# Transposes of the attention probabilities one pair at a time between the fill's matmuls, in two of a pair's four steps

## The chip, the core and the metric

The kernel runs on one core of a Trainium2 chip. The metric is the device time of one execution in microseconds (us). Before the change it is 3376.25 us, the median of 3 runs (3374.19 to 3376.97).

## What is computed

Two graph layers over x of 32 batches, each 512 rows by 512 features, all in fp32:

```python
# layer 0
y = einsum('nm,bmd->bnd', adj, x);  out = y @ weight + bias
x = layernorm(x + out)
# layer 1: masked attention with 8 heads of 64, mask = (adj == 0)
qkv  = x @ w_qkv
attn = softmax(where(mask, -inf, q @ k.T * 64**-0.5))
o    = (attn @ v) @ w_proj + b_proj
x    = layernorm(x + o + layernorm(o) * gamma + beta)
```

## The kernel before

**Number format.** Every product of two fp32 operands is done as three matmuls on parts: hi (the value rounded to fp32r) and lo (what is left), as hi·hi + hi·lo + lo·hi. ACT makes the hi parts (a copy with rounding), DVE the lo parts (a subtraction).

**Stages.** Layer 0 comes first; the first turn of layer 1 starts at 803.9 us. Layer 1 runs over 32 batches, some 79 us each. The change lies in it.

**A batch of layer 1** is four pairs of heads ("groups", 0 to 3), and each pair is four steps of 128 query rows, so a batch has 16 steps k = 0 to 15. What a step passes through, in order:

- PE `scores` (L778): q·k of both heads into `s_bank`, 6 matmuls. It stands three steps ahead: step k issues `scores(k + 3)`, which waits for `max_found` of step k + 2 (L772), since it overwrites the banks that DVE reads there.
- DVE `masked_max` (L1122): adds the mask, writes `probs` and its row maximum (`bias_row`). For step k + 2 it is issued in DVE's step k, behind `inverse(k + 1)` (L1131), which waits for `probs_turned` of step k (L1130): `probs` has two buffers, and the transposes of step k read the one that step k + 2 writes.
- ACT `exponent` (L1020), then DVE `inverse` (L1131), then POOL `normalise` (L693, L696), which counts `probs_made`.
- PE `turn` (L790 to L797): 16 transposes, in 8 pairs; the two of a pair take the upper and the lower 64 rows of the array, and write the two `t_bank`s. The last two count `probs_turned`.
- ACT `pt_hi` (L1027) and DVE `pt_lo` (L1142), two instructions each, read `t_bank`; `pt_lo` counts `ptlo_made`.
- PE `attend_v` (L813), once for the four steps of a pair: in the last step of the pair with `pt_hi`, in the first step of the next pair with `pt_lo`.

`ready_to_turn` (L783) is PE's wait before a turn: for `probs_made` of this step and `ptlo_made` of the step before. In the third and last step it stands inside `scores`, ahead of its last pair of matmuls (L775); in the first and second it stands ahead of the last matmul pair of the fill (L923).

**The fill** is work of other products that needs nothing from the current step: `v_matmuls` in group 0, `project` of the batch before in group 1, `qk_matmuls` of the next batch in groups 2 and 3. All three issue through `half_pair` (L820): one unit g is two matmuls, one in the upper and one in the lower rows of the array, lines L822 and L824. 48 units belong to a group. At g = 12 and 36 the halves of the array swap banks, so the first unit there waits until unit g - 1 is complete (L851, L872, L892). Batch 0 has no fill in group 1, the last batch none in groups 2 and 3.

PE's order is written out by hand in `batch`: the first step issues turn, matmuls with `pt_lo` and units 8 to 15, the second turn, units 16 to 25, scores, units 26 to 35, the third turn, units 36 to 47, scores, the last turn, 8 units of the next group around `pt_hi`'s matmuls, scores.

Of the kernel before, what the change touches and what calls it, by code (L numbers as in the profile page):

```python
# [18 lines left out]
def graph_layers(nc, x, adj, w0, b0, wqkv, wproj, bproj, gamma, beta, out):  # L19
    B, N, D = x.shape  # L20
    T = N // P
# [17 lines left out]
    with ExitStack() as whole:  # L39
# [474 lines left out]
        with ExitStack() as second:  # L514
# [123 lines left out]
            def pair_before(b, group):  # L638

                return (b, group - 1) if group > 0 else (b - 1, PAIRS - 1)  # L640
# [122 lines left out]
            def _(pe):  # L763
# [21 lines left out]
                    if not (isinstance(b, int) and b * STEPS + k == 0):  # L785
                        pe.wait_ge(ptlo_made, b * 32 + 2 * k)

                def turn(k):

                    for a in range(2):  # L790
                        for m in range(T):
                            for i, h in enumerate((TOP, BOTTOM)):
                                cols = slice((a * T + m) * HEAD, (a * T + m + 1) * HEAD)
                                last = pe.transpose(t_bank[i][:, cols], probs[h, k % 2, a, m * P:(m + 1) * P],  # L794
                                                    ident[h, h])
                                if a == 1 and m == T - 1:
                                    last.then_inc(probs_turned, 1)  # L797

                def attend_v(b, p, part, run):

                    first, end = part is pt_hi and run == 0, part is pt_lo and run == 0
                    if part is pt_hi and run == 0:
                        pe.wait_ge(pthi_made, b * 32 + (8 * p + 8))
                    elif part is pt_hi:
                        pe.wait_ge(pv_half, b * 16 + (4 * p + 2))
                    elif run == 1:
                        pe.wait_ge(ptlo_made, b * 32 + (8 * p + 8))
                    else:
                        pe.wait_ge(pv_half, b * 16 + (4 * p + 4))
                    for m in range(T):  # L810
                        for a, h in ((run, TOP), (1 - run, BOTTOM)):
                            w = v[h, m, 2 * p + a, :, :].rearrange("p s d -> p (s d)")
                            last = pe.matmul(o_bank[a][:], w, part[h, a, m, :], start=first and m == 0,  # L813
                                             stop=end and m == T - 1)
                            if m == T - 1 and end:
                                last.then_inc(pv_done, 1)
                            elif m == T - 1 and part is (pt_hi, pt_lo)[run]:
                                last.then_inc(pv_half, 1)
# [42 lines left out]
                def v_matmuls(b, first, count):  # L861
                    for g in range(first, first + count):
                        n, run, (m, s) = g // 24 * 2, g // 12 % 2, divmod(g % 12, 3)
                        if g % 24 == 0:
                            if isinstance(b, int) and b == 0:
                                pe.wait_ge(qklo_made, 6 + n)
                            elif n == 0:
                                pe.wait_ge(qklo_made, b * 8 + 6)
                            else:
                                pe.wait_ge(ot_summed, b * 8)  # L870
                        elif g % 12 == 0:
                            pe.wait_ge(v_half, b * 4 + (n + 2))  # L872
                        a, c = ((xt_hi, w_hi), (xt_hi, w_lo), (xt_lo, w_hi))[s]
                        pieces = half_pair([g_bank[n], g_bank[n + 1]],
                                           [a[:, m, (n + w) * P:(n + w + 1) * P] for w in range(2)],
                                           [c[:, 2, m, :]] * 2, run, g % 12 == 0, g % 12 == 11)
                        if g % 12 == 11:
                            for piece in pieces:
                                piece.then_inc(v_done if run else v_half, 1)
# [24 lines left out]
                def batch(b, last_part=True, more=True):  # L904
                    def fill(group, first, count):
                        if group == 0:
                            v_matmuls(b, first, count)
                        elif group == 1 and last_part:
                            project(b, first, count)
                        elif 2 <= group < PAIRS and more:  # L910
                            qk_matmuls(b + 1, 48 * (group - 2) + first, count)
                        elif group == PAIRS and more:
                            v_matmuls(b + 1, first, count)

                    def filled(group):
                        return group == 0 or (last_part if group == 1 else more)

                    def fill_and_wait(group, first, count, k):

                        if filled(group):  # L920
                            fill(group, first, count - 1)
                        if k < STEPS or more:
                            ready_to_turn(b + k // STEPS, k % STEPS)  # L923
                        if filled(group):
                            fill(group, first + count - 1, 1)

                    def scores_ahead(k, turn_next=False):
                        if k + 3 < STEPS or more:
                            scores(b, k + 3, (b + (k + 1) // STEPS, (k + 1) % STEPS) if turn_next else None)
                        elif turn_next and k + 1 < STEPS:  # L930
                            ready_to_turn(b, k + 1)

                    def low_outputs(b, p, between=None):
                        attend_v(b, p, pt_lo, 1)
                        if between is not None:
                            fill(*between)
                        attend_v(b, p, pt_lo, 0)

                    def first_step(k, group):
                        turn(k)  # L940
                        if group > 0 or last_part:
                            low_outputs(*pair_before(b, group), (group, 8, 2) if filled(group) else None)
                        elif filled(group):
                            fill(group, 8, 2)
                        if filled(group):
                            fill(group, 10, 2)
                        scores_ahead(k)
                        fill_and_wait(group, 12, 4, k + 1)

                    def second_step(k, group):  # L950
                        turn(k)
                        if filled(group):
                            fill(group, 16, 10)
                        scores_ahead(k)
                        fill_and_wait(group, 26, 10, k + 1)

                    def third_step(k, group):
                        turn(k)
                        if filled(group):
                            fill(group, 36, 12)  # L960
                        scores_ahead(k, turn_next=True)

                    def last_step(k, group):
                        turn(k)
                        more_fill = filled(group + 1) and (group + 1 < PAIRS or more)
                        if more_fill:
                            fill(group + 1, 0, 6)


                        if group == 0:  # L970
                            pe.wait_ge(vlo_made, b * 4 + 4)
                        elif group == 1 and last_part:
                            pe.wait_ge(o_made, b * 4)
                        elif group >= 2 and more:
                            pe.wait_ge(qklo_made, b * 8 + (4 * group + 4))
                        else:
                            pe.wait_ge(ot_summed, b * 8 + 2 * group)
                        attend_v(b, group, pt_hi, 0)
                        if more_fill:
                            fill(group + 1, 6, 2)  # L980
                        attend_v(b, group, pt_hi, 1)
                        scores_ahead(k, turn_next=True)

                    for group in range(PAIRS):
                        first_step(T * group, group)
                        second_step(T * group + 1, group)
                        third_step(T * group + 2, group)
                        last_step(T * group + 3, group)
                    if not more:
                        low_outputs(b, PAIRS - 1)  # L990
# [313 lines left out]
```

## Time and profile before

| | before |
|---|---|
| median of 3 runs | 3376.25 us |
| the profiled execution, its own time | 3375.78 us |
| its span, first to last instruction | 3374.0 us |
| PE, busy share of the span | 98% |
| DVE | 78% |
| ACT | 66% |
| POOL | 59% |
| mean granted clock of TensorE | 0.989 of 2.4 GHz |

Each row of the timeline gives a start and a duration in us from the span's start; instructions of one kind in a row are merged into one. Starts of PE's matmuls are when they are taken up, their ends are modelled: two matmuls that follow each other overlap in the rows. A step's length on PE is therefore read from the start of one turn to the start of the next.

### The profile page before, as it was taken

How to read it: one execution, taken by the hardware profiler on the slowest of the kernel's cores; microseconds unless marked ns; L12 is line 12 of the kernel's file. 1: busy time of each engine (PE TensorE's matmuls, PEld its weight loads, DVE VectorE, ACT ScalarE, POOL GpSimd, SP SyncE). 2: the span in 40 equal slices, each digit the busy share in tenths (PEclk: the TensorE clock that was granted, in tenths of full speed). 3: DMA queues.
4: the chain of work that ended last, by engine and by line, in shares of the span. 5: the costliest groups of instructions: out<-in, count | busy, mean ns of one | idle time of the engine just before them, and what ended most of it. 6: DMA issues, size and time to landing. Idle time of an engine off the chain costs nothing.

```text
span 3374.0 us, 87933 instructions
## 1 busy us (share of the span) xinstructions
PE 3308.7 (98%) x31760; PEld 2938.4 (87%) x31760; DVE 2623.3 (78%) x6430; ACT 2224.8 (66%) x4629; POOL 1991.9 (59%) x2686
## 2 busy tenths in 40 slices
PE   8999999998999999999999999999999999999995
PEld 6888888886899998999899999999999999999994
DVE  7666666664788888888888888888888888888886
ACT  4444444444677777777777777777777777777774
POOL 4555556552466666666666656666666666666665
PEclk9999999998999999999999999999999999999997
DMA  5565565553011111111122111111111111112210
GB/s 187 174 195 169 183 190 171 186 173 108 27 51 51 54 54 51 51 54 51 51 69 69 55 51 51 51 51 51 54 54 51 51 54 51 51 57 69 68 39 32
DMA packets 345168, 279.61 MB, mean 83 GB/s; under 512 B 13664, under 2 KB 275808, under 8 KB 344928
## 3 DMA queue, kind: packets, MB, share of 16 engines
q1 hardware_dynamic: 344928, 275.83, 26.8%
q8 instruction: 222, 3.64, 0.4%
q14 instruction: 18, 0.15, 0.0%
HBM read 141.56 MB, written 134.22 MB: 82 GB/s over the span
## 4 chain that ended last, share of the span: by engine, by line
PE 75%; issue 13%; POOL 9%; DVE 1%; ACT 0%; DMA 0%; SPq 0%; POOLq 0%; DVEq 0%
PE bank L822 34%; PE bank L813 15%; PE bank L778 10%; PE bank L824 9%; PE bank L794 7%; POOL xb L282 5%; POOL ub L276 4%; PE bank L319 0%; POOL rstd L287 0%; DVE probs L1122 0%; DVE o_stats L1168 0%; DVE pt_lo L1142 0%; DMA x_lo<-ut_lo 0%; ACT pt_hi L1027 0%; POOLq L279 0%
## 5 line engine op out<-in xcount | busy, mean ns | idle before, releaser
L1027 ACT ACTIVATE pt_hi<-bank 128x512 fp32r<-128x512 f32 x1024 | 556.4, 596 | 548.7 <-PE bank L794 536.0
L1020 ACT ACTIVATE probs<-probs,bias_row 128x512 f32<-128x512 f32 x1024 | 731.5, 720 | 44.8 <-DVE bias_row L1122 43.6
L1142 DVE TENSOR_TENSOR pt_lo<-bank,pt_hi 128x512 fp32r<-128x512 f32 x1024 | 657.6, 684 | 41.4 <-PE bank L813 34.4
L696 POOL TENSOR_SCALAR probs<-probs,inv_sums 128x480 f32<-128x480 f32 (+1 forms) x1024 | 685.0, 682 | 0.0
L1122 DVE CUSTOM_DVE_ANT_0 probs<-bank,mask_bias 128x512 f32<-128x512 f32 x1024 | 661.7, 683 | 9.6 <-PE bank L778 5.7
L693 POOL TENSOR_TENSOR probs<-probs,inv_sums 128x32 f32<-128x32 f32 x512 | 122.6, 239 | 734.4 <-DVE inv_sums L1131 734.3
L822 PE MATMUL bank<-x_hi,w_hi 64*128 64x512 f32 x1024 | 415.9, 406 | 7.7 <-DMA x_lo<-ut_lo 5.6
L824 PE MATMUL bank<-x_hi,w_hi 64*128 64x512 f32 x1024 | 417.6, 408 | 0.0
L794 PEld LDWEIGHTS bank<-ident,probs 64*128 64x128 f32 x8192 | 365.8, 139 | 45.0 <-issue 8.9
L822 PE MATMUL bank<-x_lo,w_hi 64*128 64x512 f32 x1024 | 403.2, 394 | 0.0
L824 PE MATMUL bank<-x_lo,w_hi 64*128 64x512 f32 x1024 | 402.9, 393 | 0.0
L824 PE MATMUL bank<-x_hi,w_lo 64*128 64x512 f32 x1024 | 398.8, 389 | 0.0
L822 PE MATMUL bank<-x_hi,w_lo 64*128 64x512 f32 x1024 | 398.5, 389 | 0.0
L794 PE MATMUL bank<-ident,probs 64*128 64x64 f32 x8192 | 352.9, 223 | 8.7 <-DVE pt_lo L1142 8.6
L1131 DVE RECIPROCAL inv_sums<-sums 128x2 f32<-128x2 f32 x512 | 83.9, 164 | 291.8 <-PE bank L794 287.4
L371 ACT ACTIVATE u<-res,shift,rstd 128x512 f32<-128x512 f32 x128 | 104.6, 817 | 306.8 <-DVE shift L454 306.8
L813 PE MATMUL bank<-pt_hi,v 64*128 64x512 f32 x2048 | 299.1, 405 | 5.4 <-ACT pt_hi L1027 5.1
L813 PE MATMUL bank<-pt_lo,v 64*128 64x512 f32 x2048 | 297.1, 402 | 0.4
L287 POOL TENSOR_TENSOR rstd<-var_eps,half_neg 128x1 f32<-128x1 f32 x128 | 95.8, 748 | 338.3 <-DVE var_eps L449 338.3
L725 POOL TENSOR_TENSOR ot_lo<-ot,ot_hi 128x512 fp32r<-128x512 f32 x127 | 164.4, 1295 | 208.8 <-ACT ot_hi L1050 208.8
L813 PEld LDWEIGHTS bank<-pt_hi,v 64*128 64x128 f32 x2048 | 207.6, 187 | 51.0 <-issue 33.3
L778 PE MATMUL bank<-k_hi,q_hi 64*128 64x512 f32 x1024 | 215.5, 390 | 8.1 <-DVE bias_row L1122 8.1
(109 smaller groups left out, 10807.4 us busy)
## 6 DMA issues: line engine op xcount, KB each, us to landing
x_in<-in_x_dram SPq DMA_DIRECT2D x32, 1024.0 KB, 5.2
u_beta_rows<-ub SPq DMA_DIRECT2D x32, 1024.0 KB, 4.4
ut_hi<-ut_hi_sb SPq DMA_DIRECT2D x128, 256.0 KB, 4.2
ut_lo<-ut_lo_sb SPq DMA_DIRECT2D x128, 256.0 KB, 3.8
x_hi<-ut_hi SPq DMA_DIRECT2D x128, 256.0 KB, 4.4
x_lo<-ut_lo SPq DMA_DIRECT2D x128, 256.0 KB, 4.7
out_dram<-o SPq DMA_DIRECT2D x128, 256.0 KB, 3.2
ub_row<-u_beta_rows SPq DMA_DIRECT2D x124, 256.0 KB, 2.7
```

Of the source, the lines that this page charges most:

```text
L282: pool.tensor_tensor(xb[:, j, :], x_in[:, j, :], b0_row[:], ALU.add).then_inc(xb_made, 1)
L696: pool.tensor_scalar(probs[:, k % 2, a, cols], probs[:, k % 2, a, cols], inv_sums[:, k % 4, a:a + 1], 0.0, ALU.mult, ALU.add)\
L725: pool.tensor_tensor(ot_lo[:, p, :], ot[:], f32(ot_hi[:, p, :]), ALU.subtract)\
L778: last = pe.matmul(s_bank[a][:], l[h, pair, n * P:(n + 1) * P], r[h, pair, :], start=i == 0, stop=i == 2)
L794: last = pe.transpose(t_bank[i][:, cols], probs[h, k % 2, a, m * P:(m + 1) * P], ident[h, h])
L813: last = pe.matmul(o_bank[a][:], w, part[h, a, m, :], start=first and m == 0, stop=end and m == T - 1)
L822: top = pe.matmul(banks[run][:], left[run][TOP], right[run][TOP], start=run == 0 and first, stop=run == 1 and end)
L824: bottom = pe.matmul(banks[1 - run][:], left[1 - run][BOTTOM], right[1 - run][BOTTOM], start=run == 0 and first, stop=run == 1 and end)
L1020: act.activation(probs[:, k % 2, a, :], probs[:, k % 2, a, :], ACT.Exp, bias=bias_row[:, k % 4, a:a + 1], scale=-1.0, accum_out=sums[:, k ...
L1027: act.activation(turned_into(pt_hi, k, i), turned(i), ACT.Copy).then_inc(pthi_made, 1)
L1122: dve.tensor_tensor_reduce(probs[:, k % 2, a, :], s_bank[a][:], mask_bias[:, k % T, :], -SCALE, 3.0e38, ALU.add, ALU.min, bias_row[:, k % ...
L1142: dve.tensor_tensor(turned_into(pt_lo, k, i), turned(i), f32(turned_into(pt_hi, k, i)), ALU.subtract).then_inc(ptlo_made, 1)
```

## The change

`turn` takes a fill function, a group and a first unit; behind each pair of transposes but the last it issues one unit of the fill. The second and third step pass it their fill, and issue the seven units fewer behind the turn. In units without a fill, and in the first and last step, nothing changes.

```diff
-                def turn(k):
+                def turn(k, fill=None, group=0, g=0):
...
                     for a in range(2):
                         for m in range(T):
...
                                 if a == 1 and m == T - 1:
                                     last.then_inc(probs_turned, 1)
+                            if fill is not None and a * T + m < 7:
+                                fill(group, g + a * T + m, 1)
...
                     def second_step(k, group):
-                        turn(k)
+                        turn(k, fill if filled(group) else None, group, 16)
                         if filled(group):
-                            fill(group, 16, 10)
+                            fill(group, 23, 3)
                         scores_ahead(k)
                         fill_and_wait(group, 26, 10, k + 1)
 
                     def third_step(k, group):
-                        turn(k)
+                        turn(k, fill if filled(group) else None, group, 36)
                         if filled(group):
-                            fill(group, 36, 12)
+                            fill(group, 43, 5)
                         scores_ahead(k, turn_next=True)
```

The number of instructions on every engine stays as it was. In the changed file the transposes of L794 stand in L795, `attend_v`'s matmuls of L813 in L816, and L822 and L824 are L825 and L827.

PE's order at the start of a second step (group 1, the fill is `project`; `ident,probs` are the transposes), before:

```order
L822 MATMUL bank<-w_hi,ot_hi 128x512 [waits ptlo_made,probs_made]
L824 MATMUL bank<-w_hi,ot_hi 128x512
L794 MATMUL bank<-ident,probs 128x64 x16
L822 MATMUL bank<-w_lo,ot_hi 128x512
L824 MATMUL bank<-w_lo,ot_hi 128x512
L822 MATMUL bank<-w_hi,ot_lo 128x512
```

and now:

```order
L825 MATMUL bank<-w_hi,ot_hi 128x512 [waits ptlo_made,probs_made]
L827 MATMUL bank<-w_hi,ot_hi 128x512
L795 MATMUL bank<-ident,probs 128x64 x2
L825 MATMUL bank<-w_lo,ot_hi 128x512
L827 MATMUL bank<-w_lo,ot_hi 128x512
L795 MATMUL bank<-ident,probs 128x64 x2
L825 MATMUL bank<-w_hi,ot_lo 128x512
L827 MATMUL bank<-w_hi,ot_lo 128x512
```

The 16 transposes, one run before, are eight runs of two with seven units between them.

PE's order in the same step from the last pair of transposes to the scores, where 20 rows of L822 and L824 stood between the two before:

```order
L795 MATMUL bank<-ident,probs 128x64 x2
L825 MATMUL bank<-w_hi,ot_lo 128x512
L827 MATMUL bank<-w_hi,ot_lo 128x512
L825 MATMUL bank<-w_hi,ot_hi 128x512 [waits ot_summed]
L827 MATMUL bank<-w_hi,ot_hi 128x512
L825 MATMUL bank<-w_lo,ot_hi 128x512
L827 MATMUL bank<-w_lo,ot_hi 128x512
L778 MATMUL bank<-k_hi,q_hi 128x512 [waits max_found,qklo_made]
```

Between the last transposes and the wait for `max_found` stand 3 units where 10 stood.

PE's order at the start of the third step (same group), before:

```order
L822 MATMUL bank<-w_hi,ot_lo 128x512 [waits ptlo_made,probs_made]
L824 MATMUL bank<-w_hi,ot_lo 128x512
L794 MATMUL bank<-ident,probs 128x64 x16
L822 MATMUL bank<-w_hi,ot_hi 128x512 [waits proj_half]
L824 MATMUL bank<-w_hi,ot_hi 128x512
```

and now:

```order
L825 MATMUL bank<-w_hi,ot_lo 128x512 [waits ptlo_made,probs_made]
L827 MATMUL bank<-w_hi,ot_lo 128x512
L795 MATMUL bank<-ident,probs 128x64 x2
L825 MATMUL bank<-w_hi,ot_hi 128x512 [waits proj_half]
L827 MATMUL bank<-w_hi,ot_hi 128x512
L795 MATMUL bank<-ident,probs 128x64 x2
```

Unit 36, which waits for unit 35 to be complete, has two transposes ahead of it instead of sixteen.

## Rows read from the trace of the kernel before

**Rows 1.** The page: busy time, share of the span, instructions.
```profile
PE 3308.7 (98%) x31760; PEld 2938.4 (87%) x31760; DVE 2623.3 (78%) x6430; ACT 2224.8 (66%) x4629; POOL 1991.9 (59%) x2686
```
**Rows 2.** Busy time by stretch; columns: all engines for the first, PE alone below.
```profile
1016.00:3200.00 2184.00, 2184.00 (x23804) 1995.86 (x23801) 1805.80 (x4631) 1641.34 (x3531) 1362.45 (x1986) 1.00 0.19 55
...
3308.45:3313.00 4.55, 2.90 (x23) 0.50 0.00 0
```
**Rows 3.** Who waited for whom, PE, whole span: us in total, times, longest.
```profile
PE bank L794 <- DVE pt_lo L1142: 8.6, 5, 3.3
PE bank L778 <- DVE bias_row L1122: 8.1, 5, 2.1
```
**Rows 4.** Timeline of PE, a third step (group 0): start, us, instruction, count.
```profile
2002.30 0.39 PE L822 MATMUL bank<-w_hi,x_lo 64*128 64x512 f32 x1
...
2002.53 0.65 PE L794 MATMUL bank<-ident,probs 64*128 64x64 f32 x15
2002.99 0.47 PE L822 MATMUL bank<-w_hi,x_hi 64*128 64x512 f32 x1
2003.00 0.22 PE L794 MATMUL bank<-ident,probs 64*128 64x64 f32 x1
...
2003.31 0.39 PE L822 MATMUL bank<-w_lo,x_hi 64*128 64x512 f32 x1
...
2005.85 0.40 PE L778 MATMUL bank<-k_hi,q_hi 64*128 64x512 f32 x2
2006.08 0.40 PE L778 MATMUL bank<-k_lo,q_hi 64*128 64x512 f32 x2
...
2006.53 0.67 PE L794 MATMUL bank<-ident,probs 64*128 64x64 f32 x16
```
**Rows 5.** Timeline of PE's weight loads at the start of that step.
```profile
2002.31 0.78 PEld L794 LDWEIGHTS bank<-ident,probs 64*128 64x128 f32 x16
```
**Rows 6.** Timeline of PE: starts of a second and of the third step after it.
```profile
2016.49 0.65 PE L794 MATMUL bank<-ident,probs 64*128 64x64 f32 x15
2022.28 0.65 PE L794 MATMUL bank<-ident,probs 64*128 64x64 f32 x15
```
**Rows 7.** Timeline of DVE, the third step of rows 4.
```profile
2003.33 0.17 DVE L1131 RECIPROCAL inv_sums<-sums 128x2 f32<-128x2 f32 x1 [1.45 <-PE bank L794]
...
2004.63 0.08 DVE L1122 DVE_READ_ACCUMULATOR2_ANT bias_row<- 128x1 f32 x1
2004.63 1.28 DVE L1142 TENSOR_TENSOR pt_lo<-bank,pt_hi 128x512 fp32r<-128x512 f32 x2
```
**Rows 8.** Timeline of POOL, the same step.
```profile
2003.79 1.34 POOL L696 TENSOR_SCALAR probs<-probs,inv_sums 128x480 f32<-128x480 f32 x2
```
**Rows 9.** Timeline of PE, last batch, group 2, which has no fill.
```profile
3300.22 2.45 PE L813 MATMUL bank<-pt_lo,v 64*128 64x512 f32 x16
3302.51 0.39 PE L778 MATMUL bank<-k_hi,q_hi 64*128 64x512 f32 x2
...
3304.40 0.71 PE L794 MATMUL bank<-ident,probs 64*128 64x64 f32 x16 [1.04 <-DVE pt_lo L1142]
3307.26 0.50 PE L778 MATMUL bank<-k_hi,q_hi 64*128 64x512 f32 x2 [2.15 <-DVE bias_row L1122]
3307.56 0.43 PE L778 MATMUL bank<-k_lo,q_hi 64*128 64x512 f32 x2
...
3308.45 1.11 PE L794 MATMUL bank<-ident,probs 64*128 64x64 f32 x16
3311.14 0.79 PE L778 MATMUL bank<-k_hi,q_hi 64*128 64x512 f32 x2 [1.57 <-DVE bias_row L1122]
```
**Rows 10.** Timeline of DVE, the same stretch.
```profile
3302.96 1.29 DVE L1142 TENSOR_TENSOR pt_lo<-bank,pt_hi 128x512 fp32r<-128x512 f32 x2
...
3305.60 0.17 DVE L1131 RECIPROCAL inv_sums<-sums 128x2 f32<-128x2 f32 x1
...
3309.71 0.17 DVE L1131 RECIPROCAL inv_sums<-sums 128x2 f32<-128x2 f32 x1
```

## Prediction

> **What bounds the kernel now.** I read the page's busy times first. PE is busy for 98% of the span, DVE for 78% [rows 1]. Then the busy time by stretch: over 2184 us of layer 1 PE is busy throughout, at the full clock of 2.4 GHz, and DVE for 1806 us of it [rows 2]. The list of waits agrees: PE's waits for DVE over the whole span are ten, 16.7 us together [rows 3], and the timeline puts them in the few steps without a fill. So PE's order sets the time. The question is what an interleaved turn costs on PE, and what becomes late behind it.
>
> Then the timeline of one filled third step [rows 4]. A pair of matmuls follows the next in 0.227 us (2005.85, 2006.08, and two pairs on to 2006.53). The step takes 4.00 us from turn to turn (2002.53 to 2006.53): a turn and 15 pairs. A second step takes 5.79 us (2016.49 to 2022.28) [rows 6]: a turn and 23 pairs.
>
> **What a turn costs.** I take it at its three joints [rows 4].
> - Into it: 2002.30 to 2002.53, 0.23 us, as between any two pairs. The transposes' weight loads had begun at 2002.31 [rows 5], under the last matmul. This joint costs nothing.
> - Within it: 15 intervals from 2002.53 to 2003.00, so 0.063 us for each pair of transposes.
> - Out of it: the unit behind is taken up at 2002.99, yet lasts 0.47 in place of 0.39 us, and the next starts at 2003.31, so this one really began 0.23 us earlier, at 3.08. The last pair of transposes began at 2.96 (its second one stands at 3.00, and they are 0.04 apart). 0.12 us. I read it as the weight load of the unit, which cannot hide under 64 columns of transpose as it does under 512 of matmul.
>
> **The change on PE alone.** Before, 7 joints of 0.063 and one of 0.12. Now a unit follows each pair of transposes, eight joints of 0.12: 7 x 0.057 = 0.40 us more per turn. In the trace of before no turn is interleaved, so both ends must be bounded. Below: the pair of transposes could vanish under its neighbours, 0 in place of 0.12. Above: I take twice 0.12. I choose 0.12, the one row that has this very order.
>
> On the weight load the Trainium skill has a rule ("TensorE: Matmul & The Clock Gate", Part 2, LDWEIGHTS): a load takes its columns divided by 1.2 GHz, for 128 columns 107 ns. Our joint of 0.12 agrees with that; the 0.063 between transposes speaks against it. With 107 ns as the joint the sum below would end 23 us lower by my estimate, which changes nothing in kind.
>
> **What becomes late.** A turn ends (I call it E) with its last pair's end. Before, E was at 2003.22 [rows 4], 0.69 us after the turn's start. Now seven units of 0.227 lie in between: the last pair starts at 7 x (0.12 + 0.227) = 2.43 us, and ends 0.26 later, E = 2.69. `probs_turned` is counted only there, so all that hangs on it moves too, while the PE work behind the turn shrinks by seven units, 1.6 us. What hangs on E, from DVE [rows 7]: its reciprocal starts at E + 0.11 (3.33), the second maximum of `masked_max` is there at E + 1.49 (4.71), `pt_lo` at E + 2.69 (5.91). ACT's `pt_hi` lies inside that. POOL has `probs` ready at 5.13, E + 1.91 [rows 8], before `pt_lo`, so `ptlo_made` is the later of the two.
>
> PE's waking from these is in the steps without a fill. From `pt_lo`'s end at 3304.25 [rows 10] to the turn at 3304.40 [rows 9]: 0.15 us. For `max_found`, E at 3309.56 to the scores at 3311.14 is 1.58 us, with DVE's reciprocal at E + 0.15 [rows 9, 10]; the earlier one is 2.15 us from E = 3305.11, but there DVE came 0.49 after E, still busy with older work. I take 1.49 + 0.15 = 1.64. The first matmul pair after such a wait holds 0.30 (3307.26 to 3307.56) in place of 0.227: 0.075 more.
>
> **Second step.** Three units behind the turn are done at 2.43 + 0.12 + 0.68 = 3.23. The scores may start at E + 1.64 = 4.33 and run from 4.41: a stall of 1.2 us, where there was none, since ten units stood there. Behind: 3 pairs of scores and 10 units, 13 x 0.227 = 2.95. Next turn at 7.35 us; `ptlo_made` (5.38) is long there. Now 5.79, so 1.56 more.
>
> **Third step.** First unit 36. It waits for unit 35. The cost of such a wait with nothing between: 16 matmuls of `attend_v`, two runs, from 3300.22 to the scores at 3302.51 take 2.29 us [rows 9], 8 pairs are 1.81, the joint out of the turn 0.12, which leaves 0.36. So unit 36 can begin 0.36 us after the turn's start, in place of 0.12: 0.24 more. Before, sixteen transposes covered this. The last pair of transposes starts at 2.67, E = 2.93. Five units end at 3.93, the scores wait for `max_found` until 4.57 + 0.075. Their last pair stands behind `ready_to_turn`, so it waits for `pt_lo`: 2.93 + 2.69 + 0.15 + 0.075 = 5.84. With its 0.227 the next turn is at 6.07. Now 4.00, so 2.07 more. Before, the slack there was under half a microsecond (5.91 against the last pair of scores, 2006.30), so this is the step with least cover.
>
> **The other two steps** I price at nothing: they follow `pt_lo` of the step before as they do now, their turns and order are unchanged, and DVE's and ACT's units of the third step come earlier in relation to E, not later, because the unit that they wait for stands nearer to the turn.
>
> **Sum.** 3.63 us per pair of heads. Filled pairs: 32 x 4, less one in batch 0 and two in the last batch, 125. 125 x 3.63 = 454 us. On the profiled execution's 3375.8 us that is 3829; its time is 0.5 us under the median, so nothing is to be added. PE's share of this is 125 x 2 x 0.40 = 100 us of slower turns, a part of which hides in the stalls; the rest is waiting.
>
> **Rivals.**
> 1. *The loads hide* (what the change's order looks made for). Joint 0.063 in place of 0.12: E at 2.29 and 2.59. Second step 2.29 + 1.64 + 0.075 + 2.95 = 6.96, third 2.59 + 3.14 = 5.73: 2.90 x 125 = 362, so 3738 us. With joints of 0: E at 1.85 and 2.21, steps 6.51 and 5.35, 259 us, so 3635. The same skill page (Part 2) says that PE pulls loads ahead of matmuls in flight; the row agrees for the load of the transposes, under a matmul [rows 5], and the joint of 0.12 speaks against it for the load after a transpose.
> 2. *Dearer changes*, joints of 0.24: 7 x 0.12 later at each E, 0.84 x 2 x 125 = 210 us more, 4039 us. For it: this order eight times over is in no row.
> 3. *The clock falls.* In the steps without a fill, with PE idle for 2.15 us, the granted clock was 0.50, which is 1.2 GHz [rows 2, 9]. Idle gaps of 1.04 us before it did not lower it. The new gaps are 1.2, 0.7 and 0.7 us. If it fell for a third of the new time, some 7 us in each group, PE's work there (about 5 us) would take some 2.5 us longer, 300 us in all: about 4130.
> 4. *Not slower.* The exposed loads go and nothing waits: each pair of transposes disappears in its unit, a turn costs 0.4 us less, 250 turns, 3276 us. It decides only if `pt_lo` were ready within 1.6 us of E, against 2.69 in the row [rows 7]. Nothing in the profile speaks for it.
>
> **How the numbers follow.** Forecast 0.74; loads hide 0.10; dearer 0.06; clock 0.07; not slower 0.03. The order shows that the change does what it says, so that is no rival. Predicted time 3829 us. The range goes down to 3700, which holds rival 1 at its likelier price, and up to 3930, half way to rival 2; outside are the rest and the clock. A measurement of this kernel can tell 0.2% from no change. Faster 0.02, within 0.2% 0.01, slower 0.97.
>
> **What would show it.** Right: PE's busy share falls to about 90%; in the list of waits PE's scores wait for DVE's `bias_row` some 250 times, by 0.6 to 1.2 us, and its last pair of scores for `pt_lo` 125 times; turns spread over 2.7 us; second steps of 7.3, third of 6.1, first and last steps still 5.0. Wrong in size: E elsewhere than 2.7 and 2.9 us after the turn's start (rivals 1 and 2), or a mean clock well under 0.98 (rival 3). Wrong in kind: no wait of PE for DVE in filled steps.

## The result, and the profile after

The changed kernel takes 3845.99 us (median of 4 runs, 3843.99 to 3847.93) against 3376.38 us before: slower, ratio 1.1391 (95% interval 1.1377 to 1.1405). The forecast was 3829 us, in a range of 3700 to 3930. The profiled execution has a span of 3842.2 us at a mean granted clock of 0.99.

The page of the changed kernel, busy time per engine:

```profile
PE 3530.5 (92%) x31760; PEld 2861.4 (74%) x31760; DVE 2622.3 (68%) x6430; ACT 2200.1 (57%) x4629; POOL 1993.6 (52%) x2686
```

DVE's, ACT's and POOL's busy times are those of [rows 1], in a longer span. PE's grew by 222 us with the same instructions. Some 80 to 100 us of this are exposed weight loads, by the runs below. The rest I read as time around the waits, which counts as busy where the modelled end of the matmul before a wait covers the wait's beginning.

Who PE waited for, changed kernel, whole span (us, times, longest):

```profile
PE bank L778 <- DVE bias_row L1125: 181.5, 255, 2.1
PE bank L778 <- DVE pt_lo L1145: 69.9, 125, 0.6
PE bank L795 <- DVE pt_lo L1145: 8.7, 6, 3.3
```

In [rows 3] the first line was 8.1 us, 5 times, and the second did not exist. 255 is 5 and twice 125: one wait in each filled second step and one in each filled third step. The lost time is more than these 251 us, because an engine counts as idle only from the modelled end of its last matmul.

The timeline of PE in the changed kernel, a second and the third step behind it:

```profile
1744.34 0.24 PE L795 MATMUL bank<-ident,probs 64*128 64x64 f32 x2
1744.37 0.48 PE L825 MATMUL bank<-w_lo,x_hi 64*128 64x512 f32 x1
...
1744.68 0.24 PE L795 MATMUL bank<-ident,probs 64*128 64x64 f32 x2
...
1746.74 0.23 PE L795 MATMUL bank<-ident,probs 64*128 64x64 f32 x2
...
1747.32 0.39 PE L825 MATMUL bank<-w_lo,x_hi 64*128 64x512 f32 x1
...
1748.75 0.50 PE L778 MATMUL bank<-k_hi,q_hi 64*128 64x512 f32 x2 [1.02 <-DVE bias_row L1125]
1749.05 0.43 PE L778 MATMUL bank<-k_lo,q_hi 64*128 64x512 f32 x2
...
1751.78 0.26 PE L795 MATMUL bank<-ident,probs 64*128 64x64 f32 x2
1752.04 0.50 PE L825 MATMUL bank<-w_hi,x_hi 64*128 64x512 f32 x1
...
1752.38 0.22 PE L795 MATMUL bank<-ident,probs 64*128 64x64 f32 x2
...
1754.45 0.22 PE L795 MATMUL bank<-ident,probs 64*128 64x64 f32 x2
...
1755.48 0.39 PE L825 MATMUL bank<-w_hi,x_lo 64*128 64x512 f32 x1
...
1756.24 0.50 PE L778 MATMUL bank<-k_hi,q_hi 64*128 64x512 f32 x2 [0.37 <-DVE bias_row L1125]
1756.58 0.40 PE L778 MATMUL bank<-k_lo,q_hi 64*128 64x512 f32 x2
1757.53 0.51 PE L778 MATMUL bank<-k_hi,q_lo 64*128 64x512 f32 x2 [0.56 <-DVE pt_lo L1145]
1757.84 0.69 PE L795 MATMUL bank<-ident,probs 64*128 64x64 f32 x16
```

What is to be seen:

- *The turn.* Pairs of transposes follow each other every 0.343 us (1744.34 to 1746.74, seven intervals). Less a unit's 0.227 that is 0.116 per joint, where 0.12 was forecast.
- *The second step's stall.* The last unit is taken up at 1747.32 and would be followed at 1747.55. The scores come at 1748.75.
- *The third step's first unit.* From the first pair of transposes to the next it is 0.60 us (1751.78 to 1752.38), 0.26 more than elsewhere: the wait of unit 36 for unit 35.
- *The third step's two stalls,* ahead of the first and ahead of the last pair of scores (0.37 and 0.56 us of idle time).
- The second step here lasts 7.44 us from turn to turn, the third 6.06. The medians over batches 2 to 29 are 7.49 and 6.05, against 5.79 and 4.00; first and last steps stayed at 4.92 to 5.04.

DVE in the same two steps:

```profile
1747.10 0.17 DVE L1134 RECIPROCAL inv_sums<-sums 128x2 f32<-128x2 f32 x1 [1.91 <-PE bank L795]
1747.29 0.69 DVE L1125 CUSTOM_DVE_ANT_0 probs<-bank,mask_bias 128x512 f32<-128x512 f32 x1
...
1748.52 0.08 DVE L1125 DVE_READ_ACCUMULATOR2_ANT bias_row<- 128x1 f32 x1
...
1754.81 0.17 DVE L1134 RECIPROCAL inv_sums<-sums 128x2 f32<-128x2 f32 x1 [3.45 <-PE bank L795]
1754.89 0.68 DVE L1125 CUSTOM_DVE_ANT_0 probs<-bank,mask_bias 128x512 f32<-128x512 f32 x1
...
1756.11 1.28 DVE L1145 TENSOR_TENSOR pt_lo<-bank,pt_hi 128x512 fp32r<-128x512 f32 x2
```

DVE is idle for 1.91 and 3.45 us and starts 0.13 and 0.14 us after a turn's end (1746.97 and 1754.67). The engine that PE then waits for had itself waited for PE. `pt_lo` ends at 1757.39, the last pair of scores follows at 1757.53.

### The profile page after: what moved, and what is told of

Read it like the earlier page. It is cut to its first block, busy times and chain, and to the rows that moved or that the text cites. A ratio compares the mean times of both kernels' runs of the same rounds, so it can differ in the third digit from the quotient of the medians.

```text
span 3842.2 us, 87933 instructions
## 1 busy us (share of the span) xinstructions
PE 3530.5 (92%) x31760; PEld 2861.4 (74%) x31760; DVE 2622.3 (68%) x6430; ACT 2200.1 (57%) x4629; POOL 1993.6 (52%) x2686
## 4 chain that ended last, share of the span: by engine, by line
PE 63%; issue 17%; DVE 10%; POOL 8%; ACT 0%; SPq 0%; DMA 0%; POOLq 0%; DVEq 0%
PE bank L825 27%; PE bank L816 13%; PE bank L778 9%; PE bank L827 8%; PE bank L795 6%; DVE pt_lo L1145 4%; POOL xb L282 4%; DVE probs L1125 3%; POOL ub L276 3%; DVE inv_sums L1134 1%; DVE bias_row L1125 1%; PE bank L319 0%; POOL rstd L287 0%; DVE o_stats L1171 0%; DVEq L1133 0%
## 5 line engine op out<-in xcount | busy, mean ns | idle before, releaser
L795 PE MATMUL bank<-ident,probs 64*128 64x64 f32 x8192 | 645.3, 219 | 8.7 <-DVE pt_lo L1145 8.7
L795 PEld LDWEIGHTS bank<-ident,probs 64*128 64x128 f32 x8192 | 495.9, 139 | 33.6 <-issue 9.1
L825 PE MATMUL bank<-x_hi,w_hi 64*128 64x512 f32 x1024 | 436.2, 426 | 9.3 <-DMA x_lo<-ut_lo 5.7
L827 PE MATMUL bank<-x_hi,w_hi 64*128 64x512 f32 x1024 | 438.7, 428 | 0.0
L825 PE MATMUL bank<-x_lo,w_hi 64*128 64x512 f32 x1024 | 430.9, 421 | 0.0
L827 PE MATMUL bank<-x_lo,w_hi 64*128 64x512 f32 x1024 | 430.6, 421 | 0.0
L825 PE MATMUL bank<-x_hi,w_lo 64*128 64x512 f32 x1024 | 426.0, 416 | 0.0
L827 PE MATMUL bank<-x_hi,w_lo 64*128 64x512 f32 x1024 | 425.0, 415 | 0.0
L778 PE MATMUL bank<-k_hi,q_hi 64*128 64x512 f32 x1024 | 232.2, 439 | 181.5 <-DVE bias_row L1125 181.5
L778 PEld LDWEIGHTS bank<-k_hi,q_hi 64*128 64x128 f32 x1024 | 103.5, 184 | 294.4 <-issue 182.6
L816 PE MATMUL bank<-pt_hi,v 64*128 64x512 f32 x2048 | 299.0, 406 | 5.3 <-ACT pt_hi L1030 5.1
L816 PE MATMUL bank<-pt_lo,v 64*128 64x512 f32 x2048 | 294.0, 402 | 0.3
L778 PE MATMUL bank<-k_hi,q_lo 64*128 64x512 f32 x1024 | 223.1, 414 | 70.0 <-DVE pt_lo L1145 69.9
```

The source lines that it names most:

```text
L778: last = pe.matmul(s_bank[a][:], l[h, pair, n * P:(n + 1) * P], r[h, pair, :], start=i == 0, stop=i == 2)
L825: top = pe.matmul(banks[run][:], left[run][TOP], right[run][TOP], start=run == 0 and first, stop=run == 1 and end)
L827: bottom = pe.matmul(banks[1 - run][:], left[1 - run][BOTTOM], right[1 - run][BOTTOM], start=run == 0 and first, stop=run == 1 and end)
```

## The experiments

Theory A is the forecast's: the turn's end comes late, less work is left behind it to cover DVE's chain, and the joints are dearer. Its rival B puts the cost on PE alone, the same for each of the 14 interleaved units. Every experiment is timed against the kernel before, on the same chip.

### One step at a time

The change in the second steps alone:

```diff
                     def third_step(k, group):
-                        turn(k, fill if filled(group) else None, group, 36)
+                        turn(k)
                         if filled(group):
-                            fill(group, 43, 5)
+                            fill(group, 36, 12)
```

> The change in the second steps alone; the third steps as before. Theory A (a late end of the turn takes away the cover of DVE's chain, plus dearer joints between transposes and units): second steps keep their 7.49 us of the changed kernel against 5.79, third steps return to 4.00, so 125 x 1.70 = 212 us over before: 3589 us. Theory B (the cost is on PE alone, in equal parts for each of the 14 interleaved units, 3.75 / 14 = 0.27 us each): 125 x 7 x 0.27 = 234 us, 3611 us. Theory C (the steps push each other: a third step is slow because the second one was): third steps stay above 4.00, up to 6.05, and the time lies between 3600 and 3845.

Measured: 3586.36 us, ratio 1.0621 (1.0605 to 1.0638), 209 us over the kernel before. Second steps 7.47 to 7.48 us, third steps 3.98. C falls: a third step is not slow because of the second. The time is 3 us under A's figure and 25 under B's, but a cost on PE in unequal parts would fit it too, so A and B are not told apart by this.

The change in the third steps alone (second step as before, `turn(k)` and `fill(group, 16, 10)`):

> The change in the third steps alone; the second steps as before. Theory A: third steps keep 6.05 us against 4.00, second steps are back at 5.79: 125 x 2.05 = 256 us over before, 3633 us; together with the second-only run (+209 us) that is the whole change (+469 us). If the two steps' costs were not independent, the sum would miss by more than 10 us.

Measured: 3631.25 us, ratio 1.0755 (1.0738 to 1.0771), 255 us. The two add up to 464 us, the whole change is 470. The steps' costs are independent within 6 us.

### The late turn without the interleaving

```diff
                     def second_step(k, group):
-                        turn(k, fill if filled(group) else None, group, 16)
+                        if filled(group):
+                            fill(group, 16, 7)
+                        turn(k)
                         if filled(group):
                             fill(group, 23, 3)
```

and the same in the third step with `fill(group, 36, 7)`; `turn` is one run of 16 again.

> The same seven units stand ahead of a turn in one piece instead of between its pairs, in the second and third steps. No joint between transposes and matmuls is added; the turn ends late as in the change, less the dearer joints. Theory A: second step 7 x 0.227 + 0.69 = 2.28 to the turn's end, then 1.64 + 0.075 + 13 x 0.23, so 7.0 us (+1.2); third step 0.36 + 1.59 + 0.69 = 2.64, then 3.12, so 5.8 us (+1.8): 3.0 x 125 = 375 us, 3751 us. Theory B (joints on PE alone): nothing is added, 3376 us.

Measured: 3768.41 us, ratio 1.1161 (1.1143 to 1.1178), 391 us, where A had said 375 and B none. This is the run that decides. With no joint added, 391 of the 470 us are there. PE's waits in it:

```profile
PE bank L778 <- DVE bias_row L1129: 181.3, 255, 2.1
PE bank L778 <- DVE pt_lo L1149: 69.9, 125, 0.6
```

They are those of the changed kernel to 0.2 us. So the waits come from where the turn's end stands, and not from what the turn looks like inside. The rest, 469.6 - 391.5 = 78 us or 0.63 us per pair of heads, is left for the joints; 14 x 0.057 = 0.80 was their forecast, but this variant pays 0.12 us of its own, since unit 36 follows unit 35 directly (0.36 us more than a unit's 0.227, against 0.24 in the change, medians of the traces). 0.63 + 0.12 = 0.75.

### The interleaving with its cover given back

Second steps alone, all seven units in the turn, and twelve units between the turn and the scores:

```diff
                     def second_step(k, group):
                         turn(k, fill if filled(group) else None, group, 16)
                         if filled(group):
-                            fill(group, 23, 3)
+                            fill(group, 23, 12)
                         scores_ahead(k)
-                        fill_and_wait(group, 26, 10, k + 1)
+                        fill_and_wait(group, 35, 1, k + 1)
```

> Second steps alone are interleaved, and nine of the ten units behind the scores are moved ahead of them, so twelve units lie between the last transposes and the wait for the row maximum. Theory A: no wait for DVE in second steps; what is left are seven dearer joints, 7 x 0.057 = 0.40 us a step, 6.19 us in place of 5.79: 125 x 0.40 = 50 us, 3426 us. Theory B: the units cost the same as without the cover, 7.49 us a step, 3589 us or so. Were the joints free, 3376 us.

Measured: 3485.89 us, ratio 1.0321 (1.0306 to 1.0337), 109 us: neither 50 nor 212. The second steps are what A said, 6.18 to 6.19 us in the medians of the groups, and PE's waits for `bias_row` are back at 5. But 30 waits for `pt_lo` are new ahead of the last pair of scores, 16.8 us in all. The other 59 us are in steps that the edit does not touch: third steps of 4.19 us in groups 0 and 3 and 4.97 in group 2, first and last steps of up to 5.27. One third step of group 2, PE:

```profile
1681.37 0.65 PE L795 MATMUL bank<-ident,probs 64*128 64x64 f32 x15
1681.83 0.22 PE L795 MATMUL bank<-ident,probs 64*128 64x64 f32 x1
...
1685.06 0.40 PE L778 MATMUL bank<-k_lo,q_hi 64*128 64x512 f32 x2
1686.01 0.50 PE L778 MATMUL bank<-k_hi,q_lo 64*128 64x512 f32 x2 [0.56 <-DVE pt_lo L1145]
```

and DVE:

```profile
1681.52 0.68 DVE L1151 TENSOR_TENSOR k_lo<-bank,k_hi 128x512 fp32r<-128x512 f32 x1
1682.12 0.69 DVE L1171 BATCH_NORM_STATS2 o_stats<-o 128x6 f32<-128x512 f32 x1
...
1683.29 0.17 DVE L1134 RECIPROCAL inv_sums<-sums 128x2 f32<-128x2 f32 x1
```

The third turn ends at 1682.05, but DVE takes up its chain 1.24 us later, at 1683.29, with no idle time ahead. It is still busy with the second step's work, which could only begin at that step's late turn end. Between the two turn ends lie 4.2 us here (6.19 - 2.67 + 0.69), where they were 5.8 us before, and DVE's row statistics of group 2 do not fit. In group 3 (and by the medians in group 0) it is ACT that is late. The third turn ends at 1703.24, but ACT's `pt_hi` stands behind output rows that it scales (L1058), without idle time ahead, and starts 1.17 us later. DVE's `pt_lo` waits for it:

```profile
1702.99 1.52 ACT L1058 ACTIVATE o<-o,o_shift,o_rstd 128x512 f32<-128x512 f32 x2
1704.41 1.07 ACT L1030 ACTIVATE pt_hi<-bank 128x512 fp32r<-128x512 f32 x2
...
1705.03 1.29 DVE L1145 TENSOR_TENSOR pt_lo<-bank,pt_hi 128x512 fp32r<-128x512 f32 x2 [0.26 <-ACT pt_hi L1030]
```

A late end takes from both sides: cover on PE behind it, and room on DVE and ACT before the next one. What counts for the second is the distance between two ends. In the run with the change in second steps alone the third steps were not pushed (3.98 us), since the second step had grown with its late end: 7.48 - 2.65 + 0.68 = 5.5 us lie between the ends there, and 7.7 in the change itself.

### Fewer units in the turn

As above, but a unit behind the second, fourth and sixth pair of transposes only, and sixteen ahead of the scores:

```diff
-                            if fill is not None and a * T + m < 7:
-                                fill(group, g + a * T + m, 1)
+                            if fill is not None and a * T + m in (1, 3, 5):
+                                fill(group, g + (a * T + m) // 2, 1)
```

> As the covered one, but a unit stands behind every second pair of transposes (three units in the turn, in place of seven). Theory A, with joints that add up one by one: 3 x 0.057 = 0.17 us a step, 5.96 us: 125 x 0.17 = 21 us, 3398 us. If only the first joint of a turn cost something, or if each change of kind shifted the following matmuls too, it would lie nearer to the covered one with seven units (3426 us).

Measured: 3398.32 us, ratio 1.0064 (1.0051 to 1.0078), 21 us. Second steps 5.97 us, the others within 0.04 us of before. Three joints cost 0.18 us where seven had cost 0.40, so they add up one by one. The scores stand behind nineteen units of the step in both runs and start at nearly the same place (5.06 us after the turn's start here, 5.28 in the covered run; medians), so it was not their place that made its third steps slow, but the turn's end: 1.52 us after its start here, 2.65 there.

A unit behind the second and fourth pair, eight units (18 to 25) ahead of the scores, none moved past them:

> Second steps alone, a unit behind the second and the fourth pair of transposes, eight units left between the last pair and the scores, none moved past the scores. Theory A: the turn ends at 2 x (0.12 + 0.23) + 4 x 0.063 + ... = about 1.26 us, the scores are reached at 2.96 and may start at 2.90, so nothing waits; only two dearer joints, 2 x 0.057 = 0.11 us a step: 125 x 0.11 = 14 us, 3391 us. Theory B (each interleaved unit costs 1.70 / 7 = 0.24 us): 2 x 0.24 x 125 = 61 us, 3438 us.

Measured: 3409.01 us, ratio 1.0095 (1.0080 to 1.0111), 33 us, between the two theories. PE around the scores of a second step:

```profile
1995.01 0.22 PE L795 MATMUL bank<-ident,probs 64*128 64x64 f32 x1
...
1996.71 0.39 PE L825 MATMUL bank<-x_lo,w_hi 64*128 64x512 f32 x1
...
1996.99 0.50 PE L778 MATMUL bank<-k_hi,q_hi 64*128 64x512 f32 x2
1997.30 0.42 PE L778 MATMUL bank<-k_lo,q_hi 64*128 64x512 f32 x2
```

The turn ends at 1995.23, the scores come 1.76 us later, not 1.64. They are 0.05 us late behind the last unit, and their first pair holds 0.31 in place of 0.227. That is 0.13 us of waiting and 0.11 of joints, 0.24 x 125 = 30 us. A's mechanism holds; its threshold was 0.12 us too low. No wait is listed for it, as the last matmul's modelled end hides it.

### What the joint is

The kernel before, without interleaving, but unit 27 of each group cut into eight pieces of 64 columns, each with its own weight load:

```diff
+                    if narrow:
+                        for n in range(8):
+                            c = slice(n * HEAD, (n + 1) * HEAD)
+                            top = pe.matmul(banks[run][:, c], left[run][TOP], right[run][TOP, c],
+                                            start=False, stop=False)
...
+                        return top, bottom
```

> The kernel before, with unit 27 of each group cut into eight pieces of 64 columns, each with its own weight load, same values. It measures the pitch at which the fill's weights can be loaded when no long matmul covers them. If the joint of 0.12 us behind a transpose is the load of the unit's weights, the eight pieces follow each other in about 0.12 us: 128 x (8 x 0.12 - 0.23 + 0) = 93 us, 3470 us. If the joint is the price of a change of kind (transpose to matmul) and fill weights load as fast as those of the transposes (0.063 us), 128 x (8 x 0.063 - 0.23) = 35 us, 3412 us, plus one slower joint at the end of each at most.

Measured: 3467.95 us, ratio 1.0269 (1.0253 to 1.0285), 92 us. The pieces:

```profile
1717.58 0.27 PE L824 MATMUL bank<-w_hi,x_hi 64*128 64x64 f32 x1
...
1717.69 0.27 PE L824 MATMUL bank<-w_hi,x_hi 64*128 64x64 f32 x1
...
1718.25 0.27 PE L824 MATMUL bank<-w_hi,x_hi 64*128 64x64 f32 x1
```

The last seven of the eight stand 0.112 us apart (1717.58 to 1718.25, six intervals). The same unit in four pieces of 128 columns:

> As the run with unit 27 in eight pieces, but four pieces of 128 columns. The eight pieces of 64 columns had followed each other in 0.112 us. If the weight load is what sets that pitch (the columns hide under it), it stays 0.112 us with twice the columns: 4 x 0.112 - 0.23 + 0.09 late start of what follows = about 0.22 us a unit is the whole step's increase less the pieces' own hidden part, a time of 3376 + 128 x (0.45 - 0.23) = 3404 us. If the pitch is a fixed price per matmul plus its columns (0.085 + 64 / 2400), it becomes 0.139 us: 128 x (0.556 - 0.23) = 42 us, 3418 us.

Measured: 3406.31 us, ratio 1.0087 (1.0071 to 1.0103), 30 us.

```profile
1715.06 0.27 PE L824 MATMUL bank<-w_hi,ot_hi 64*128 64x128 f32 x1
...
1715.17 0.27 PE L824 MATMUL bank<-w_hi,ot_hi 64*128 64x128 f32 x1
...
1715.29 0.27 PE L824 MATMUL bank<-w_hi,ot_hi 64*128 64x128 f32 x1
```

0.115 us, nearly the same with twice the columns, where a price per column had asked for 0.139. So the columns do not set the pitch, and no transpose is near. What each piece has, in each half of the array, is one weight load of 128 columns in fp32r. These loads, in the run with eight pieces, stand as far apart as the pieces:

```profile
1717.67 0.19 PEld L824 LDWEIGHTS bank<-w_hi,x_hi 64*128 64x128 f32 x1
...
1717.78 0.19 PEld L824 LDWEIGHTS bank<-w_hi,x_hi 64*128 64x128 f32 x1
```

I take the load to be what takes the 0.112 us, and the joint of 0.116 behind a transpose to be this load, bare. No run changes the size of a load, so a fixed price of the same size for each load and matmul of this kind is not excluded. The transposes' own loads, fp32, follow each other in 0.063 us, as [rows 4] showed. The interleaving uncovered seven more of the dear kind and covered seven of the cheap kind.

### The other direction

If the cover behind a turn is what counts, units should go to where the slack is smallest. The last and first step of the kernel before start two of their matmuls slightly late, behind waits for `pt_hi` and `pt_lo`. One unit moved from the second into the last step:

```diff
-                            fill(group, 16, 10)
+                            fill(group, 17, 9)
...
-                            fill(group + 1, 0, 6)
+                            fill(group + 1, 0, 7)
...
-                            fill(group + 1, 6, 2)
+                            fill(group + 1, 7, 2)
```

with the first step's units beginning at 9 accordingly.

> No interleaving. The kernel before, with one unit of the fill moved from the second step to the last step, where seven units in place of six stand between the turn and the first matmuls with pt_hi, which start 0.02 to 0.1 us late there. If that small wait is real, it goes, and 128 x 0.1 = up to 12 us are gained: 3365 us. If the order of PE is full already and the slow start there is no wait, no difference: 3377 us.

Measured: 3367.17 us, ratio 0.9972 (0.9960 to 0.9983), 9 us less than before. One more into the first step:

```diff
-                        fill_and_wait(group, 12, 5, k + 1)
+                        fill_and_wait(group, 12, 6, k + 1)
...
-                            fill(group, 17, 9)
+                            fill(group, 18, 9)
...
-                        fill_and_wait(group, 26, 10, k + 1)
+                        fill_and_wait(group, 27, 9, k + 1)
```

> The kernel with the unit moved into the last step (3367 us), and one unit more of the fill moved from the second step into the first, behind the scores, where PE's wait for pt_lo stands ahead of the last unit. If the late start there (0.26 us from the unit that waits to the one before, in place of 0.227, and 0.30 to the turn) is a wait, 0.05 to 0.07 us a step go: 3358 to 3361 us. If not, 3367 us.

Measured: 3354.09 us, ratio 0.9935 (0.9920 to 0.9949), 22 us less than before and more than expected. It is the fastest version of this study. Its turns, from a last step on:

```profile
1702.14 0.68 PE L794 MATMUL bank<-ident,probs 64*128 64x64 f32 x16
...
1707.30 0.66 PE L794 MATMUL bank<-ident,probs 64*128 64x64 f32 x16
...
1712.41 0.67 PE L794 MATMUL bank<-ident,probs 64*128 64x64 f32 x16
...
1717.76 0.69 PE L794 MATMUL bank<-ident,probs 64*128 64x64 f32 x16
```

The last step takes 5.16 us, the first 5.11, the second 5.35, where they were 5.02, about 5.0 and 5.79. A batch shrank by some 0.7 us (79.3 to 78.6, medians).

The forecast for the second move, 3358 to 3361 us, was missed. The medians by group show where the rest comes from. From the run before to this one the first step took in a unit of 0.227 us and grew by 0.17, 0.21, 0.10 and 0.12 us in groups 0 to 3. So the late start was 0.02 to 0.13 us, and larger in groups 2 and 3 than the 0.05 to 0.07 of the expectation. The second step gave a unit up and shrank by 0.24 to 0.26. Together that is about 0.4 us a batch, or 12 of the 13 us between the two runs.

## Why the prediction was right

- *What bounds the kernel:* PE's order, with DVE's chain close behind it. Right: with PE's order moved, DVE's chain became the bound in two of four steps. The count of PE's waits for DVE was short: beside the ten, 16.7 us, the list of before has two more, for `ut_lo_sb` (2.0 us) and `ot_lo` (1.5 us). Nothing hangs on them.
- *The joint:* 0.12 us taken from the one row of that order; 0.116 measured. The account given with it, the unit's weight load, was tested as far as this: the same unit's loads and matmuls follow each other in 0.112 us with no transpose near, whatever the columns.
- *The turn's end:* 2.69 and 2.93 us after the turn's start forecast; the last pairs start at 2.40 and 2.67 in the rows above and end 0.23 and 0.22 us later, 2.63 and 2.89.
- *The second step:* 7.35 forecast, 7.49 measured. The term that was too small is the 1.64 us from the turn's end to the scores. The scores came 1.78 us after the end (1746.97 to 1748.75), 0.14 more. DVE's first maximum starts 0.19 us after its reciprocal in second steps (1747.10 to 1747.29), and 0.08 in third ones (1754.81 to 1754.89), from which I had read the chain. The second steps of the kernel before have the longer distance already:

```profile
2017.38 0.17 DVE L1131 RECIPROCAL inv_sums<-sums 128x2 f32<-128x2 f32 x1
2017.57 0.69 DVE L1122 CUSTOM_DVE_ANT_0 probs<-bank,mask_bias 128x512 f32<-128x512 f32 x1
```

- *The third step:* 6.07 forecast, 6.05 measured, with the extra of unit 36 at 0.26 in the rows (0.24 in the median) against 0.24. Here the 1.64 us were too long, 1.57 in the medians, without effect: the step's end hangs on the later wait, for `pt_lo`.
- *The sum:* 17 us short. 0.14 us in the second step, less 0.02 in the third, are 15 of them, 125 times; 0.02 us in the last step (5.04 against 5.02) are the other two. That it came so near is in part luck, as errors cancel: in second steps the turn's end came 0.04 us early, and the stretch from the scores to the next turn took 3.07 us in place of 3.02.
- *Steps priced at nothing:* right for the change, 4.92 to 5.04 us as before. The reason that I gave does not cover every late end: the covered run shows that a second turn that ends late, in a step that does not grow with it, pushes the steps behind it.
- *The rivals:* the loads do not hide behind a transpose (0.116 us, not 0.063), the changes are not dearer than 0.12, the granted clock stayed at 0.99 in the mean, and the time went the way that was forecast. Of PE's own the forecast had 100 us; the run with the units ahead of the turn leaves 78 to 94 for it, the rest is waiting.

## What to carry to other kernels

An instruction stream that is full still has a shape: what another engine waits for should end early, and the work that nobody waits for belongs behind it, not in between. Before interleaving, read two intervals in the trace: from the signal's last instruction to the first wait that depends on it, and the length of the chain in between; their difference is all that may be moved. And look at what covers each weight load: here a transpose of 64 columns was no cover for the load of the next matmul, and each change from one to the other cost 0.057 us more than the next transpose would have.

## What the runs showed that I had not expected

- Weight loads of 128 columns in fp32r follow each other in 0.112 us where no long matmul covers them (a pair of row halves), those of the fp32 transposes, of the same size, in 0.063 us. On the first the Trainium skill ("TensorE: Matmul & The Clock Gate", Part 2, LDWEIGHTS: columns divided by 1.2 GHz, 107 ns) agrees with the trace; for the second the measurement decides.
- PE's idle gaps of up to 1.02 us in every second and third step did not lower its granted clock: 1.00 from 1016 to 3200 us, and 0.99 in the mean over the span, as before.
- A wait of 0.13 us on PE is in no list of waits; it shows only as 0.31 us between two pairs of matmuls that should stand 0.227 apart.
